# A fused LoRA and routed-adapter layer: A0's transposes, Bx's steps and a weight load change places in the prologue

## The chip, the cores and the metric

One core of a Trainium2 chip runs the kernel as one program. The metric is device time in microseconds (us). The profiled execution is a separate one, taken by the hardware profiler; its times are from the start of its span.

## The reference

x is 8 batches of 512 tokens by 2048, in float32. Two residual layers follow each other:

```
Bx  = x @ B0[adapter[b]].T                    # rank 16
x   = x + Bx @ A0[adapter[b]].T               # layer 0, a LoRA adapter chosen per batch
base   = x @ W.T                              # layer 1, W is 2048 x 2048
logits = x @ Wr.T + 5 * one_hot(language[b])  # 8 experts
gates  = softmax over the top 2 logits
h      = x @ A.T                              # 8 experts x rank 16 = 128 columns
x   = x + base + 2 * (h * gates) @ B.T
```

## The kernel before, in words

**How products are made.** Every float32 operand of a product is split into a high part (ScalarE casts it to fp32r) and a low part (VectorE subtracts), and TensorE sums three products of the parts (high by high, low by high, high by low; L820 to L822). TensorE's work for one batch is a list of slots, one for each pair of W's blocks. Batch 0 has 36 slots and works straight from W; batches 1 to 7 use sums of blocks that the slots of batch 0 prepare and store.

**The order is written by hand.** Each engine executes its own list of steps: `pe_start`, `act_start`, `dve_start`, `pool_start` and `sp_start` are the prologue, and `pe_main` and its fellows the slots. Engines meet only at semaphores, and an instruction that waits holds back all that stands behind it on its engine. SyncE (`sp_start`, `sp_main`) issues nearly all loads.

**The prologue.** It transposes x of batch 0 on TensorE in sixteen units (`x_transpose`, L319), ScalarE and VectorE take turns in copying a unit out of PSUM (`x_keep_act` L325, `x_keep_dve` L330), then `x_hi` (L350) and `x_lo` (L355) split it, and `aux_products` (L378, L380) multiplies it by the 152 columns of A, Wr and B0. The loop variable s in the lists is the step: at step s TensorE transposes unit 4 + s and multiplies unit s, while ScalarE and VectorE split unit 3 + s. After the last unit the sum of its second half is read (`aux_low` L390, `aux_sum` L395), and the sixteen columns of Bx go through `bx_hi` (L400, L401), `bx_lo` (L405), `bx_transpose` (L417) and `bx_keep` (L426), which leaves Bx in `bxt`.

**A0's part.** GpSimd orders A0 into `a0p`. `a0_transpose` 0 to 3 turns it (L1121), `a0_copy` (L1126, ScalarE) leaves it in `a0t`. `a0_rows_hi` (L1142, ScalarE) and `a0_rows_lo` (L1147, VectorE) split these rows in two halves; SyncE then sends the rows of batch 0 to `a0g` with three DMAs (L1407) and all rows to `a_scr` in memory with two (L1409). `a0_transpose` 4 to 7, `a0_hi` (L1131) and `a0_lo` (L1135) give the operand of `g_products` (L1157), sixteen tiles that multiply A0 by the same 152 columns.

**The first update of x.** `delta` (L533) is the product of `bxt` and `a0g` for one unit; it waits for `bxt` and for the rows in `a0g`. `adapt` (L540, VectorE) adds it to x, `first_hi` (L553) and `first_lo` (L558, called xl in the rows) split the new x. In slots 0 to 6 VectorE makes units 4 to 15 in this way, one or two in a slot. In the slots of batch 0 VectorE also turns a pair of W (`w_turn` L684, and L691 for blocks on the diagonal), forms two block sums (`w_sums`), and makes the low part of a pair (`pair_lo` L816) after ScalarE's high part (`pair_hi` L812). `first_products` of slot i waits for `pair_lo` of pair i, and at even i for units of `first_lo`. A pair of W is loaded by `first_load` (L669). GpSimd stores turned pairs and sums (`w_store`, `w_sums_store`), copies the second adapter's B into `bnj` (L1348), and makes two more block sums of each pair.

Of the kernel before, what the change touches and what calls it, by code (L numbers as in the profile page):

```python
# [5 lines left out]
def adapted_moe_lora_kernel(nc, x, adapter_ids, language_ids, A0, B0, W, Wr, A, Bm, out):  # L6
# [82 lines left out]
    with ctx:  # L89
# [1049 lines left out]
        def a0_rows_hi(e, half):  # L1139
            cols = slice(half * HO, (half + 1) * HO)  # L1140
            e.wait_ge(c_ac, 4)
            e.copy(arh[:, cols].bitcast(f32r), a0t[:, cols]).then_inc(c_arh, 1)  # L1142
# [79 lines left out]
        def pe_start(e):  # L1222
            warm(e, 18)
            for u in range(2):
                x_transpose(e, u)
            warm(e, 4)
            for m in range(2):
                a_transpose(e, m)
            small_transpose(e)
            for u in range(2, 4):  # L1230
                x_transpose(e, u)
            for s in range(16):
                if s < 12:
                    x_transpose(e, 4 + s)
                aux_products(e, 0, s)
                if 1 <= s < 3:
                    a_transpose(e, 1 + s)
                if 8 <= s < 16:
                    a0_transpose(e, s - 8)
            g_products(e, range(7))  # L1240
            bx_transpose(e, 0)
            g_products(e, range(7, 11))
            for u in range(2):
                delta(e, 0, u)
            g_products(e, range(11, 16))
            for u in range(2, 4):
                delta(e, 0, u)

        def act_start(e):
            x_load(e, 0, 0)  # L1250
            x_keep_act(e, 0)
            for u in range(2):
                x_hi(e, 0, u)
            for m in range(2):
                a_hi(e, m)
            small_hi(e)
            x_keep_act(e, 2)
            x_hi(e, 0, 2)
            for s in range(15):
                if s < 12 and s % 2 == 0:  # L1260
                    x_keep_act(e, 4 + s)
                if s == 8:
                    aux_low(e, 0, 0)
                if s < 13:
                    x_hi(e, 0, 3 + s)
                if 1 <= s < 3:
                    a_hi(e, 1 + s)
                if 8 <= s < 12:
                    a0_copy(e, s - 8)
                if s in (12, 13):  # L1270
                    a0_rows_hi(e, s - 12)
                if 12 <= s < 15:
                    a0_hi(e, s - 12)
                if s == 13:
                    pair_hi(e, 0)
            aux_low(e, 0, 1)
            a0_hi(e, 3)
            bx_hi(e, 0)
            pair_hi(e, 1)
            bx_keep(e, 0)  # L1280
            for u in range(2):
                first_hi(e, u)
            g_low(e)
            for u in range(2, 4):
                first_hi(e, u)
            g_hi(e)

        def dve_start(e):
            x_keep_dve(e, 1)
            for u in range(2):  # L1290
                x_lo(e, 0, u)
            for m in range(2):
                a_lo(e, m)
            small_lo(e)
            x_keep_dve(e, 3)
            x_lo(e, 0, 2)
            for s in range(15):
                if s < 12 and s % 2:
                    x_keep_dve(e, 4 + s)
                if s == 8:  # L1300
                    aux_sum(e, 0, 0)
                if s < 13:
                    x_lo(e, 0, 3 + s)
                if 1 <= s < 3:
                    a_lo(e, 1 + s)
                if s == 9:
                    bias_columns(e)
                if s in (12, 13):
                    a0_rows_lo(e, s - 12)
                if 12 <= s < 15:  # L1310
                    a0_lo(e, s - 12)
                if s in (9, 11):
                    w_turn(e, (s - 9) // 2)
            pair_lo(e, 0)
            aux_sum(e, 0, 1)
            a0_lo(e, 3)
            bx_lo(e, 0)
            w_sums(e, 0)
            pair_lo(e, 1)
            for u in range(2):  # L1320
                adapt(e, 0, u)
            for u in range(2):
                first_lo(e, u)
            for u in range(2, 4):
                adapt(e, 0, u)
            for u in range(2, 4):
                first_lo(e, u)
            g_sum(e)
            g_lo(e)
            w_turn(e, 2)  # L1330
            w_sums(e, 1)
# [43 lines left out]
        def sp_start(e):  # L1375
# [24 lines left out]
                first_load(e, g)  # L1400
            e.wait_ge(c_tr, 8)
            e.dma_start(bn, Bm.rearrange("e (p j) r -> p e j r", p=P)).then_inc(d_bn, 16)
            first_load(e, 3)
            e.wait_ge(c_ar, 2)
            e.wait_ge(c_pool, 5)
            for row, part in G_ROWS:
                e.dma_start(a0g[row:row + R, 0:D].bitcast(f32), (arh, arl)[part][0:R, :]).then_inc(d_ar, 16)  # L1407
            for s, t in enumerate((arh, arl)):
                e.dma_start(a_scr[s, :, 0:D], t).then_inc(d_as, 16)  # L1409
            first_load(e, 4)  # L1410
# [326 lines left out]
```

## Time and profile before

| | |
|---|---|
| median of 3 runs | 1571.99 us (1569.66 to 1574.66) |
| the profiled execution, its time | 1573.06 us |
| its span | 1571.3 us |
| TensorE busy | 1546.0 us (98%) |
| VectorE busy | 1225.4 us (78%) |
| ScalarE busy | 713.4 us (45%) |
| GpSimd busy | 138.9 us (9%) |
| granted TensorE clock, mean | 0.996 |
| bytes moved | 347.05 MB, 221 GB/s |

Busy time is the time in which an engine has an instruction under way; matmuls are pipelined, so a busy TensorE is not one at its peak. In a row of a timeline a square bracket gives the idle time of the engine ahead of the instruction and who ended it. The start of one instruction may lie up to 0.1 us ahead of the end of the one before it.

### The profile page before, as it was taken

Reading aid. Unit: us, or ns where it says so; the run is one execution under the profiler, and the core shown is the slowest. Engines: PE = TensorE matmul, PEld = TensorE weight load, DVE = VectorE, ACT = ScalarE, POOL = GpSimd, SP = SyncE. Lnnn points to the kernel's source line nnn. Section 1 sums busy time; section 2 is a strip of 40 time slices with the busy share of each in tenths; the row PEclk is TensorE's granted clock in tenths of the full one; section 3 lists DMA queues with packets and bytes.
Section 4 is the critical chain, followed back from the end, with each engine's and each line's share of the span. In section 5 each row is a group of like instructions: output and inputs, shape, how many; then the busy total and the mean of one; then the engine's idle time right before and its main releaser. Section 6 shows DMA issues by size and latency. Waiting matters only on the chain.

```text
span 1571.3 us, 20339 instructions
## 1 busy us (share of the span) xinstructions
PE 1546.0 (98%) x7430; PEld 1298.4 (83%) x7430; DVE 1225.4 (78%) x1630; ACT 713.4 (45%) x911; POOL 138.9 (9%) x181
## 2 busy tenths in 40 slices
PE   9989999999999999999999999999999999999998
PEld 9768877888888888888888888888888888888887
DVE  6987768877699777997688876987769976787665
ACT  6422222445445444454444544454444554445443
POOL 2565545000000000000000000000000000000000
PEclk9999999999999999999999999999999999999999
DMA  9799999687767777777776886668776786666664
GB/s 258 201 245 292 261 230 249 211 251 202 224 218 205 227 200 232 228 218 206 213 228 206 239 219 208 220 202 240 208 221 215 211 234 196 204 225 212 202 216 160
DMA packets 303110, 347.05 MB, mean 221 GB/s; under 512 B 204890, under 2 KB 236682, under 8 KB 302346
## 3 DMA queue, kind: packets, MB, share of 16 engines
q1 hardware_dynamic: 293602, 314.28, 69.1%
q0 software_dynamic: 9136, 30.94, 6.2%
q8 instruction: 59, 0.97, 0.3%
q10 hardware_dynamic: 272, 0.52, 0.1%
q14 instruction: 41, 0.34, 0.1%
HBM read 278.52 MB, written 66.72 MB: 220 GB/s over the span
## 4 chain that ended last, share of the span: by engine, by line
PE 90%; DVE 5%; DMA 2%; ACT 1%; issue 1%; SPq 1%; POOL 0%; DVEq 0%; ACTq 0%; POOLq 0%
PE pb L820 27%; PE pb L821 27%; PE pb L822 26%; PE pb L378 4%; PE pb L380 4%; PE pb L533 2%; DVE raw L684 1%; DVE xl L558 1%; DVE wl L816 1%; ACT wh L812 1%; DVE pool_a L540 1%; DMA t_scr<-ost 0%; DMA an<-in_L_cond_A_dram 0%; DMA raw<-in_L_cond_W_dram 0%; PE pb L319 0%
## 5 line engine op out<-in xcount | busy, mean ns | idle before, releaser
L812 ACT CAST wh<-raw 128x1024 fp32r<-128x1024 f32 (+1 forms) x453 | 475.1, 1049 | 716.9 <-PE pb L822 689.1
L816 DVE TENSOR_TENSOR wl<-raw,wh 128x1024 fp32r<-128x1024 f32 (+1 forms) x453 | 558.2, 1232 | 275.4 <-ACT wh L812 274.4
L820 PE MATMUL pb<-wh,sh 128*128 128x512 f32 x1568 | 612.9, 391 | 0.5 <-DVE ost L870 0.5
L821 PE MATMUL pb<-wl,sh 128*128 128x512 f32 x1568 | 611.7, 390 | 0.0
L822 PE MATMUL pb<-wh,sl 128*128 128x512 f32 x1568 | 611.1, 390 | 0.0
L822 PEld LDWEIGHTS pb<-wh,sl 128*128 128x128 f32 x1568 | 294.3, 188 | 62.9
L820 PEld LDWEIGHTS pb<-wh,sh 128*128 128x128 f32 x1568 | 294.5, 188 | 56.4 <-DVE wl L816 0.9
L821 PEld LDWEIGHTS pb<-wl,sh 128*128 128x128 f32 x1568 | 294.6, 188 | 55.0
L378 PE MATMUL pb<-awb,xah 128*128 128x304 f32 x512 | 139.3, 305 | 0.9 <-DVE xal L355 0.9
L380 PE MATMUL pb<-awb,xal 128*128 128x256 f32 x512 | 134.9, 280 | 0.0
L820 PE MATMUL pb<-wh,xh 128*128 128x512 f32 x256 | 102.2, 399 | 7.4 <-DVE xl L558 5.6
L378 PEld LDWEIGHTS pb<-awb,xah 128*128 128x128 f32 x512 | 96.9, 189 | 5.7 <-issue 1.3
L821 PE MATMUL pb<-wl,xh 128*128 128x512 f32 x256 | 101.1, 395 | 0.0
L822 PE MATMUL pb<-wh,xl 128*128 128x512 f32 x256 | 101.1, 395 | 0.0
L380 PEld LDWEIGHTS pb<-awb,xal 128*128 128x128 f32 x512 | 96.9, 189 | 4.1
L610 DVE TENSOR_TENSOR sl<-pool_a,sh 128x512 fp32r<-128x512 f32 x120 | 83.1, 693 | 0.3
L605 ACT CAST sh<-pool_a 128x512 fp32r<-128x512 f32 x120 | 73.5, 613 | 0.0
L350 ACT CAST xah<-pool_a 128x512 fp32r<-128x512 f32 x88 | 54.6, 621 | 28.8 <-DVE pool_a L277 27.9
L355 DVE TENSOR_TENSOR xal<-pool_a,xah 128x512 fp32r<-128x512 f32 x88 | 61.5, 699 | 3.5 <-ACT xah L350 3.3
L820 PEld LDWEIGHTS pb<-wh,xh 128*128 128x128 f32 x256 | 48.9, 191 | 18.1 <-DVE xl L558 4.0
L540 DVE TENSOR_TENSOR pool_a<-pool_a,pb 128x512 f32<-128x512 f32 x88 | 58.3, 677 | 1.0 <-PE pb L533 1.0
L533 PEld LDWEIGHTS pb<-bxt,a0g 128*128 128x128 f32 x256 | 45.1, 188 | 16.9 <-DVE pool_a L540 5.1
(155 smaller groups left out, 1298.0 us busy)
## 6 DMA issues: line engine op xcount, KB each, us to landing
raw<-t_scr SPq DMA_DIRECT2D x392, 512.0 KB, 3.9
xst<-in_x_dram SPq DMA_DIRECT2D x448, 64.0 KB, 3.9
out_dram<-ost SPq DMA_DIRECT2D x72, 256.0 KB, 3.6
raw<-in_L_cond_W_dram SPq DMA_DIRECT2D x124, 128.0 KB, 5.0
raw<-bt_scr SPq DMA_DIRECT2D x28, 512.0 KB, 3.6
out_dram<-u SPq DMA_DIRECT2D x56, 256.0 KB, 2.8
t_scr<-raw POOLq DMA_DIRECT2D x32, 256.0 KB, 4.6
t_scr<-tst POOLq DMA_DIRECT2D x16, 512.0 KB, 6.2
```

The source lines that it names most:

```text
L355: e.tensor_tensor(out=x_low(n, u).rearrange("p k t -> p (k t)"), in0=two(n, q, kp), in1=x_high(n, u).rearrange("p k t -> p (k t)").bitcast ...
L378: e.matmul(pb[:, aux_bank(n, u // 8) + t, 0:2 * AW], x_high(n, u)[:, k, toks], cols[:, 0:2 * AW], start=u % 8 == 0 and k == 0, stop=False)
L380: last = e.matmul(pb[:, aux_bank(n, u // 8) + t, 0:LOW], x_low(n, u)[:, k, toks], cols[:, 0:LOW], start=False, stop=u % 8 == 7 and k == 1)
L533: last = e.matmul(pb[:, delta_bank(n, u), k * HT:(k + 1) * HT], a0g[:, at:at + P], bxt[:, q // 2 * HT:(q // 2 + 1) * HT], start=True, stop ...
L540: e.tensor_tensor(out=two(n, q, kp), in0=two(n, q, kp), in1=pb[:, delta_bank(n, u), :], op=ALU.add)\
L605: e.copy(sh[:, h % SR, :, :].rearrange("p k t -> p (k t)"), two(b, SUM_QUARTER[product], kp)).then_inc(c_sph, 1)
L610: e.tensor_tensor(out=sl[:, h % SR, :, :].rearrange("p k t -> p (k t)"), in0=two(b, SUM_QUARTER[product], kp), in1=sh[:, h % SR, :, :].rea ...
L812: e.copy(pair_split(wh, g), pair_source(g)).then_inc(c_wh, 1)
L816: e.tensor_tensor(out=pair_split(wl, g), in0=pair_source(g), in1=pair_split(wh, g).bitcast(f32), op=ALU.subtract).then_inc(c_wl, 1)
L820: e.matmul(o, h, wh[:, g % RING, k, :], start=start, stop=False)
L821: e.matmul(o, h, wl[:, g % RING, k, :], start=False, stop=False)
L822: return e.matmul(o, l, wh[:, g % RING, k, :], start=False, stop=stop)
```

## The change

No instruction is added or taken away; instructions change places in four lists.

- TensorE: the eight groups of A0's transposes come at steps 5 to 8 and 10 to 13 instead of 8 to 15. `bx_transpose` comes after four tiles of `g_products` instead of seven, and the first two `delta` after eight instead of eleven.
- ScalarE: A0's copies and the splits of its rows move three steps ahead, `a0_hi` two or more. `pair_hi(0)` moves from step 13 to after the last step, still ahead of `aux_low(0, 1)`; `bx_keep` comes ahead of `pair_hi(1)`.
- VectorE: the splits of A0's rows move three steps ahead, `a0_lo` two or more. `w_turn` of pairs 0 and 1 moves from steps 9 and 11 to 12 and 14, `bias_columns` from step 9 to after the first `pair_lo`, `pair_lo(0)` to behind `bx_lo`, `pair_lo(1)` to behind the second two `adapt`, `w_sums(0)` to behind the fourth `first_lo`.
- SyncE: the load of pair 3 of W goes behind the rows of A0 and stands ahead of that of pair 4.

```diff
--- before.py
+++ after.py
@@ -1235,14 +1235,16 @@
                 aux_products(e, 0, s)
                 if 1 <= s < 3:
                     a_transpose(e, 1 + s)
-                if 8 <= s < 16:
-                    a0_transpose(e, s - 8)
-            g_products(e, range(7))
+                if 5 <= s < 9:
+                    a0_transpose(e, s - 5)
+                if 10 <= s < 14:
+                    a0_transpose(e, s - 6)
+            g_products(e, range(4))
             bx_transpose(e, 0)
-            g_products(e, range(7, 11))
+            g_products(e, range(4, 8))
             for u in range(2):
                 delta(e, 0, u)
-            g_products(e, range(11, 16))
+            g_products(e, range(8, 16))
             for u in range(2, 4):
                 delta(e, 0, u)
 
@@ -1265,19 +1267,17 @@
                     x_hi(e, 0, 3 + s)
                 if 1 <= s < 3:
                     a_hi(e, 1 + s)
-                if 8 <= s < 12:
-                    a0_copy(e, s - 8)
-                if s in (12, 13):
-                    a0_rows_hi(e, s - 12)
-                if 12 <= s < 15:
-                    a0_hi(e, s - 12)
-                if s == 13:
-                    pair_hi(e, 0)
+                if 5 <= s < 9:
+                    a0_copy(e, s - 5)
+                if s in (9, 10):
+                    a0_rows_hi(e, s - 9)
+                if 10 <= s < 14:
+                    a0_hi(e, s - 10)
+            pair_hi(e, 0)
             aux_low(e, 0, 1)
-            a0_hi(e, 3)
             bx_hi(e, 0)
+            bx_keep(e, 0)
             pair_hi(e, 1)
-            bx_keep(e, 0)
             for u in range(2):
                 first_hi(e, u)
             g_low(e)
@@ -1303,28 +1303,26 @@
                     x_lo(e, 0, 3 + s)
                 if 1 <= s < 3:
                     a_lo(e, 1 + s)
-                if s == 9:
-                    bias_columns(e)
-                if s in (12, 13):
-                    a0_rows_lo(e, s - 12)
-                if 12 <= s < 15:
-                    a0_lo(e, s - 12)
-                if s in (9, 11):
-                    w_turn(e, (s - 9) // 2)
+                if s in (9, 10):
+                    a0_rows_lo(e, s - 9)
+                if 10 <= s < 14:
+                    a0_lo(e, s - 10)
+                if s in (12, 14):
+                    w_turn(e, (s - 12) // 2)
+            aux_sum(e, 0, 1)
+            bx_lo(e, 0)
             pair_lo(e, 0)
-            aux_sum(e, 0, 1)
-            a0_lo(e, 3)
-            bx_lo(e, 0)
-            w_sums(e, 0)
-            pair_lo(e, 1)
+            bias_columns(e)
             for u in range(2):
                 adapt(e, 0, u)
             for u in range(2):
                 first_lo(e, u)
             for u in range(2, 4):
                 adapt(e, 0, u)
+            pair_lo(e, 1)
             for u in range(2, 4):
                 first_lo(e, u)
+            w_sums(e, 0)
             g_sum(e)
             g_lo(e)
             w_turn(e, 2)
@@ -1400,11 +1398,11 @@
                 first_load(e, g)
             e.wait_ge(c_tr, 8)
             e.dma_start(bn, Bm.rearrange("e (p j) r -> p e j r", p=P)).then_inc(d_bn, 16)
-            first_load(e, 3)
             e.wait_ge(c_ar, 2)
             e.wait_ge(c_pool, 5)
             for row, part in G_ROWS:
                 e.dma_start(a0g[row:row + R, 0:D].bitcast(f32), (arh, arl)[part][0:R, :]).then_inc(d_ar, 16)
+            first_load(e, 3)
             for s, t in enumerate((arh, arl)):
                 e.dma_start(a_scr[s, :, 0:D], t).then_inc(d_as, 16)
             first_load(e, 4)
```

## Rows read from the trace of the kernel before

**Rows 1.** The chain that ended last, piece from 42 us

```profile
42.02 5.08 DMA a0g<-a0p
```

**Rows 2.** Timeline of TensorE, 0 to 106 us: start, us, engine, line, operation [idle before]

```profile
22.69 0.63 PE L319 MATMUL pb<-ident,xst 128*128 128x128 f32 x4
...
24.18 0.63 PE L319 MATMUL pb<-ident,xst 128*128 128x128 f32 x4
...
28.68 0.60 PE L1121 MATMUL pb<-ident,a0p 128*128 128x128 f32 x4
...
30.62 0.60 PE L1121 MATMUL pb<-ident,a0p 128*128 128x128 f32 x4
...
41.75 0.39 PE L1157 MATMUL pb<-awb,a0h 128*128 128x304 f32 x1
...
44.23 0.66 PE L417 MATMUL pb<-ident,st 128*128 128x128 f32 x4 [0.28 <-DVE st L405]
...
47.24 0.71 PE L533 MATMUL pb<-bxt,a0g 128*128 128x256 f32 x4 [1.24 <-DMA a0g<-a0p]
...
50.56 0.47 PE L820 MATMUL pb<-wh,xh 128*128 128x512 f32 x1 [0.76 <-DVE xl L558]
...
84.14 0.52 PE L820 MATMUL pb<-wh,xh 128*128 128x512 f32 x1 [2.54 <-DVE xl L558]
...
103.78 0.50 PE L820 MATMUL pb<-wh,xh 128*128 128x512 f32 x1 [0.85 <-DVE xl L558]
```

**Rows 3.** Timeline of VectorE, 19 to 57 us

```profile
19.52 1.18 DVE L355 TENSOR_TENSOR xal<-pool_a,xah 128x512 fp32r<-128x512 f32 x1 [0.32 <-ACT xah L350]
...
25.99 0.69 DVE L355 TENSOR_TENSOR xal<-pool_a,xah 128x512 fp32r<-128x512 f32 x1 [1.11 <-ACT xah L350]
...
28.78 0.47 DVE L395 TENSOR_TENSOR aux<-pb,auxl 128x304 f32<-128x304 f32 x1 [0.90 <-ACT auxl L390]
...
30.97 0.69 DVE L355 TENSOR_TENSOR xal<-pool_a,xah 128x512 fp32r<-128x512 f32 x1 [0.38 <-ACT xah L350]
31.58 0.17 DVE L1215 CAST lidf<-lid 128x8 f32<-128x8 int32 x1
...
32.15 1.30 DVE L684 STREAM_TRANSPOSE raw<-raw 128x512 f32<-128x512 f32 x2
33.37 0.45 DVE L691 TENSOR_TENSOR raw<-raw,ident 128x128 f32<-128x128 f32 x2
...
37.74 1.22 DVE L1147 TENSOR_TENSOR a0p<-a0t,a0n 128x1024 fp32r<-128x1024 f32 x1
...
42.98 0.46 DVE L395 TENSOR_TENSOR aux<-pb,auxl 128x304 f32<-128x304 f32 x1
...
47.75 1.28 DVE L540 TENSOR_TENSOR pool_a<-pool_a,pb 128x512 f32<-128x512 f32 x2 [0.98 <-PE pb L533]
...
56.21 1.55 DVE L816 TENSOR_TENSOR wl<-raw,wh 128x1024 fp32r<-128x1024 f32 x1 [0.35 <-ACT wh L812]
```

**Rows 4.** Timeline of ScalarE, 29 to 46 us

```profile
29.32 1.20 ACT L1126 COPY a0t<-pb 128x512 f32<-128x512 f32 x1
30.25 0.69 ACT L350 CAST xah<-pool_a 128x512 fp32r<-128x512 f32 x1
...
36.62 1.05 ACT L1142 CAST a0n<-a0t 128x1024 fp32r<-128x1024 f32 x1
...
44.92 0.59 ACT L426 CAST bxt<-pb 128x512 fp32r<-128x512 f32 x1
```

**Rows 5.** SyncE's queue, 40 to 42 us

```profile
40.71 1.26 SPq L1407 DMA_DIRECT2D a0g<-a0n  x2
```

**Rows 6.** Timeline of GpSimd, 38 to 44 us

```profile
38.78 4.88 POOL L1348 COPY xst<-ost 128x256 f32<-128x256 f32 x8
```

**Rows 7.** Windows of TensorE in slots 3 and 4: busy us, granted clock, DMA share, GB/s

```profile
83.00:86.00 3.00, 1.86 (x5) 0.75 1.07 252
86.00:89.00 3.00, 3.00 (x11) 0.69 0.75 186
```

## The prediction

> **What bounds the kernel now.** I read the page first, then the chain that ended last, then the timelines of the five engines up to 106 us, and last the windows. The page says that TensorE is busy 98% of the span, so a change in the first 50 us can only shift the point from which it is always busy. The chain shows what sets that point. Up to 42 us it runs through the splits of A0's rows on VectorE and SyncE's queue, then through the landing of these rows [rows 1], and TensorE stands 1.24 us before the first delta [rows 2]. From there on it is VectorE's list, with short pieces of ScalarE: adapt, first_lo, w_turn, pair_lo, slot after slot. VectorE has no long idle time between 56 and 104 us; the typical one is the 0.35 us before a pair_lo [rows 3]. TensorE, which starts its slots at 50.56, is made to wait for xl 2.54 us at 84.14 and 0.85 us at 103.78 [rows 2]. After that last wait TensorE sets the pace. So what matters is not when the first delta starts but how late VectorE is when it leaves the prologue, which I read at its pair_lo of slot 0, 56.21 us [rows 3]. TensorE may be early or late by up to about 2.5 us in between; 84.14 takes it out.
>
> The same instructions run before and after on VectorE. So the result is a ledger of VectorE's idle time: whatever idle the new order adds ahead of that pair_lo is added to the end, whatever it removes is won. In before, from 24.8 us on, the idle times are 1.11, 0.90, 0.38 and 0.98 us [rows 3], 3.4 in all; the short ones after 50 us I take as common to both.
>
> **Prices.** A step of TensorE with transposes of x takes 1.49 us (22.69 to 24.18), one with A0's too 1.94 (28.68 to 30.62), so a group of A0's is 0.45 [rows 2]. VectorE: two instructions of 512 columns 1.30, so 0.61 apiece start to start; a w_turn with its two additions 1.6 (32.15 to 33.8); bias_columns 0.57 (31.58 to 32.15); 1024 columns 1.22, so about 1.13 start to start [rows 3]. ScalarE: a0_copy 0.93 (29.32 to 30.25), 512 columns about 0.5, 1024 columns about 0.95 [rows 4]. An engine sees another's result some 0.05 to 0.2 us after its end: a0_copy started at 29.32, the group of transposes having ended about 29.13.
>
> **Steps 5 to 8: A0's transposes and copies, three units sooner.** The first group starts at 24.18, where unit 10 was transposed [rows 2], and ends at 24.63. Four steps of 1.94 follow instead of 1.49; step 9 starts at 30.45. ScalarE takes the first copy at 24.8 and holds it to 25.75, the copy of unit 10 to 26.25, and only then x_hi of unit 9, complete at 26.85. VectorE waits for it from 24.8 to 26.9: 2.0 us idle after taking off the usual gap, where before it had 1.11. The next x_lo comes at 28.4, 0.3 idle. ScalarE's third copy runs 28.7 to 29.63, so aux_low comes at 30.15 and aux_sum at 30.6: 1.55 idle where it was 0.90. At these steps VectorE has 0.9 us of work in 1.94 and nothing to fill the rest. In before the longer steps were 8 to 11, and there w_turn and bias_columns filled them. This is the cost of the change.
>
> **Steps 9 to 14.** Steps 9 to 11 of TensorE end at 31.95, 33.9 and 35.8. ScalarE's a0_rows_hi run at 32.4 and 34.4, each behind an x_hi. VectorE's a0_rows_lo follow at 33.5 and 35.5 and end at 36.65; it waits 0.25 us each for x_lo of unit 12 and the two row halves, 0.7 together where it had 0.38. Then it has work without a break: a0_lo 0 to 37.3, the copy of unit 15 to 37.9, x_lo 14, a0_lo 1 to 39.1, x_lo 15 to 39.65, a0_lo 2 to 40.25, w_turn 0 to 41.85, a0_lo 3 to 42.45, w_turn 1 to 44.05. TensorE waits for a0_lo twice, about 0.55 and 0.25 us, and ends the sixteenth unit near 41.75, where the g_products started in before [rows 2]; the earlier A0 gives it nothing there.
>
> **The steps of Bx.** ScalarE has pair_hi(0) ahead of aux_low, and pair_hi(0) waits for w_turn 0 until 41.9: aux_low is complete at 43.35. VectorE is free of w_turn 1 only at 44.05, so aux_sum starts at 44.05 instead of 42.98. What follows is shorter, as a0_lo 3 no longer stands in it: bx_hi 44.55, bx_lo 45.0 (VectorE idle 0.5), bx_transpose 45.27 against 44.23, bx_keep 45.97 against 44.92, bxt complete at 46.6 against 45.51 [rows 2 to 4]. Behind bx_transpose stand four tiles of g_products, 1.1 us, to 46.8. The first delta is then at 46.8 instead of 47.24, 0.45 sooner.
>
> **The rows of A0 and pair 3.** SyncE gets both row halves at 36.7 instead of 40.71 [rows 5], 4 us sooner. The third DMA, 1.3 us on, would land at about 43.1 by the 5.08 us of before [rows 1]; even two more would do, as bxt comes at 46.6. So the wait of 1.24 us is gone, but bxt's lateness takes most of it. Pair 3 of W is loaded after the two stores to a_scr, and when w_turn 0 is done: about 41.9 to 44.6. It is wanted in slot 0 at some 63 us, so I cost this move at nothing; the bound above is small too, as 10 us of landing would still be in time. Pair 4 starts about 44.6, where it started 45.3. The sums of pair 0, a slot's worth later, are stored by GpSimd near 55 us; GpSimd then waits for w_turn 2 and the sums of pair 1 as before, and its last sum of pair 1 is ready near 60, ahead of w_turn 3. Nothing there is late.
>
> **VectorE up to slot 0.** From bx_lo: pair_lo(0) 45.15 to 46.3, bias_columns to 46.9, a wait of 0.35 for the delta, two adapt from 47.3 to 48.5, two first_lo to 49.9, a wait of 0.2 (TensorE has eight tiles of g_products, 2.25 us, ahead of the next two delta), two adapt to 51.35, pair_lo(1) to 52.5, two first_lo to 53.7, w_sums(0) to 55.15, the two steps of g to 56.0, w_turn 2 to 57.25, w_sums(1) to 58.05, and with the usual gap pair_lo at 58.45. It was 56.21. The ledger agrees: idle 2.0 + 0.3 + 1.55 + 0.7 + 0.5 + 0.35 + 0.2 = 5.6 us against 3.4, so VectorE is 2.2 us later. The 0.45 us gained at the delta is inside this: VectorE had idle time there, and now has work that it should have done earlier.
>
> **What covers it.** TensorE's first products need first_lo 0 and 1, at 49.9 against 50.3, and its second half first_lo 3, near 53.7 where it arrived at 53.9 before. So slot 0 starts as early as ever. But units 6 and 7 are 2.2 us late when TensorE wants them near 69 us, and the wait at 84.14 ends 2.2 us later. No slot from there to 103.78 has spare time on VectorE, so it all reaches the end: **+2.2 us**. On the profiled execution this is 1573.06 + 2.2 = 1575.3; on the median, 1.07 below that execution, 1571.99 + 2.2 = **1574.2 us**. A difference of 0.3%, 4.7 us, is about what a measurement of this kernel can tell from no change, so I forecast the same time, on the slow side of it.
>
> **The port of GpSimd, by row and rule.** The eight copies of B took GpSimd 38.78 to 43.66 [rows 6]. They wait behind the store of pair 1, which now follows w_turn 1, so they run 45.4 to 50.3, beside pair_lo(0) and two first_lo. An x_lo that ran beside a copy of GpSimd took 1.18 instead of 0.69 us [rows 3]. Three such meetings would cost 1.5 us; but the a0_rows_lo at 37.74 ran into the first of the eight and took 1.22, its ordinary length, so below the bound is 0. I take 0, since those are the same copies. The Trainium skill (GPSIMD Engine Reference, section Specifications) says that GpSimd shares its SBUF interfaces with VectorE and contends with VectorE instructions that have two SBUF inputs. By it the three would be slowed and the two adapt, with one input in PSUM, would not; the sum would be about 1575.7 on the median, and the row at 19.52 bears it out in part.
>
> **Rivals.** (1) *The gain reaches the end.* If ScalarE does not hold up x_hi in steps 5 to 8 (copies shorter, or VectorE's later waits for ScalarE short), the ledger ends level and the 0.98 us idle before the first adapt is what is removed: 1.0 to 1.2 us less, 1571.0. For it: the chain names the landing, 5.08 us of it [rows 1]. Against it: ScalarE's 0.93 us copy stands ahead of x_hi in its list, whatever else happens. (2) *The port*, as above: 0.5 to 1.5 us more, 1575. (3) *TensorE's clock falls, the case on the slow side.* TensorE now stands from 42.9 to 45.3 for bx_transpose, 2.4 us, since it has only four tiles to fill with. After the wait of 2.54 us the granted clock was 0.75 and 0.69 in two stretches of 3 us [rows 7]: it fell to half, 1.2 GHz, for 3.4 us of the six (0.25 and 0.31 lost, over 0.5), which costs 1.7 us of matmul work. Here the delta and g_products would carry it, VectorE waits for delta 2 until about 52, and is 1.8 us later again: +4.0, 1576.0. It passes 0.3% if the low stretch lasts longer than 4.8 us. For it: the similar wait. Against: 2.4 is shorter, and 1.24 us of waiting left the clock alone. (4) *The change does nothing*: the moved steps fall into idle time everywhere and the end stays, 1572.
>
> **How the numbers follow.** Forecast 0.5; (1) 0.18; (2) 0.12; (3) 0.12, half of whose weight is near or over the 0.3% line; (4) 0.08. The range reaches from (1) to beyond (3), widened by 1.5 us for the scatter of the median, which moved 5 us over three runs: 1569.6 to 1577.4. Slower by over 0.3% needs 1576.7: 0.09. Faster needs 1567.3, for which I find no mechanism, as all idle time that could go is 3.4 us: 0.03. The same: 0.88.
>
> **What the profile will show.** Right: VectorE's idle time before x_lo of unit 9 near 2 us and before aux_sum above 1.2; no wait of TensorE on the rows of A0; first delta near 46.8; pair_lo of slot 0 near 58.4; the wait of 2.5 us at 86.3. Wrong: that pair_lo at 56.2 or earlier means that the ledger was misread; a granted clock below 1 between 44 and 50 us means rival 3; first_lo above 1 us in the prologue, rival 2. If pair 3 arrived late there would be a VectorE wait on a load near 63 us.

## The result and the profile after

The changed kernel takes 1575.89 us, the median of 20 runs (1573.28 to 1580.73), against 1572.26 us for the kernel before (20 runs, 1569.13 to 1574.66). The ratio is 1.0026, with a 95% interval of 1.0020 to 1.0032: 3.6 us slower by the medians and 4.1 by the ratio, inside the 0.3% (4.7 us) that the prediction called no change, and on the side that it named. Its forecast was 2.2 us.

The profiled execution of the changed kernel has a span of 1573.8 us. TensorE's timeline, from the transposes of unit 9 and A0's first group, now behind them:

```profile
20.70 0.63 PE L319 MATMUL pb<-ident,xst 128*128 128x128 f32 x4
...
22.19 0.60 PE L1121 MATMUL pb<-ident,a0p 128*128 128x128 f32 x4
...
43.52 0.66 PE L417 MATMUL pb<-ident,st 128*128 128x128 f32 x4 [2.43 <-DVE st L405]
...
45.89 1.06 PE L533 MATMUL pb<-bxt,a0g 128*128 128x256 f32 x4
...
49.86 0.40 PE L820 MATMUL pb<-wh,xh 128*128 128x512 f32 x1
```

```profile
62.92 0.66 PE L1184 MATMUL pb<-ident,xst 128*128 128x128 f32 x4 [3.17 <-ACT bt L1189]
...
86.40 0.50 PE L820 MATMUL pb<-wh,xh 128*128 128x512 f32 x1 [2.53 <-DVE xl L558]
```

The wait for the rows of A0 is gone (45.89 has no bracket), and a wait of 2.43 us for bx_lo has come. The one in slot 4 has the length it had, 2.53 us, and ends 2.26 us later than in [rows 2] by the time of each trace. The wait of 3.17 us at 62.92 is new; ScalarE's copy of bt stands behind a first_hi that is late there. It is gone by 86.40, where TensorE waits for VectorE anyway.

VectorE's timeline, with lines that answer to [rows 3]:

```profile
24.96 0.69 DVE L355 TENSOR_TENSOR xal<-pool_a,xah 128x512 fp32r<-128x512 f32 x1 [1.42 <-ACT xah L350]
...
28.65 0.47 DVE L395 TENSOR_TENSOR aux<-pb,auxl 128x304 f32<-128x304 f32 x1 [1.48 <-ACT auxl L390]
...
30.69 0.69 DVE L355 TENSOR_TENSOR xal<-pool_a,xah 128x512 fp32r<-128x512 f32 x1 [0.24 <-ACT xah L350]
31.64 1.23 DVE L1147 TENSOR_TENSOR a0p<-a0t,a0n 128x1024 fp32r<-128x1024 f32 x1 [0.25 <-ACT a0n L1142]
...
38.32 1.30 DVE L684 STREAM_TRANSPOSE raw<-raw 128x512 f32<-128x512 f32 x2
...
40.51 1.30 DVE L684 STREAM_TRANSPOSE raw<-raw 128x512 f32<-128x512 f32 x2
...
42.10 0.47 DVE L395 TENSOR_TENSOR aux<-pb,auxl 128x304 f32<-128x304 f32 x1
43.03 0.44 DVE L405 TENSOR_TENSOR st<-aux,st 128x64 f32<-128x64 f32 x1 [0.46 <-ACT st L401]
43.39 1.42 DVE L816 TENSOR_TENSOR wl<-raw,wh 128x1024 fp32r<-128x1024 f32 x1
44.73 0.36 DVE L1215 CAST lidf<-lid 128x8 f32<-128x8 int32 x1
45.13 0.35 DVE L1217 TENSOR_TENSOR bias<-iota,lidf 128x64 f32<-128x64 f32 x1
45.52 0.28 DVE L1220 TENSOR_SCALAR bias<-bias 128x64 f32<-128x64 f32 x1
46.56 1.29 DVE L540 TENSOR_TENSOR pool_a<-pool_a,pb 128x512 f32<-128x512 f32 x2 [0.75 <-PE pb L533]
...
49.83 1.28 DVE L540 TENSOR_TENSOR pool_a<-pool_a,pb 128x512 f32<-128x512 f32 x2 [0.60 <-PE pb L533]
...
55.50 0.71 DVE L1176 TENSOR_TENSOR late<-late 128x136 fp32r<-128x136 f32 x1 [0.37 <-ACT late L1172]
...
58.54 1.55 DVE L816 TENSOR_TENSOR wl<-raw,wh 128x1024 fp32r<-128x1024 f32 x1 [0.35 <-ACT wh L812]
```

The idle times ahead of x_lo of unit 9 (24.96) and of aux_sum (28.65) have grown from 1.11 and 0.90 us to 1.42 and 1.48, the turns of pairs 0 and 1 run at 38.32 and 40.51 where they ran from 32.15, and the second aux_sum follows them at once. Behind it, bx_lo, pair_lo(0) and bias_columns (43.03 to 45.80) are all longer than the same instructions were, and each pair of adapt waits for its delta.

SyncE's queue and GpSimd's copies and next instruction, as in [rows 5, 6]:

```profile
34.84 1.26 SPq L1404 DMA_DIRECT2D a0g<-a0n  x2
...
40.03 1.91 SPq L669 DMA_DIRECT2D raw<-in_L_cond_W_dram  x4
41.98 0.60 SPq L1407 DMA_DIRECT2D a_scr<-a0n  x1
```

```profile
43.75 3.71 POOL L1346 COPY xst<-ost 128x256 f32<-128x256 f32 x8
...
55.98 0.82 POOL L738 TENSOR_TENSOR ost<-raw 128x256 f32<-128x256 f32 x1
```

The rows of A0 are sent 5.9 us sooner than in before (3.9 by the count from unit 9 that follows, where 4 was forecast), pair 3 goes out at 40.03 when w_turn 0 is done, and the copies of B start at 43.75 instead of 38.78, on top of bx_lo and pair_lo(0).

**One correction for how these two traces are compared.** Both kernels are the same up to the transposes of unit 9 in step 5, but the profiled execution of before had TensorE at half clock in step 0 and part of step 1 and that of the changed kernel had not. The windows of before and of after, from 13 to 16 us, with busy time of TensorE, granted clock, DMA share and GB/s:

```profile
13.00:16.00 3.00, 3.00 (x16) 0.50 1.08 360
```

```profile
13.00:16.00 3.00, 3.00 (x27) 1.00 1.08 362
...
44.00:46.00 2.00, 2.00 (x11) 0.55 1.09 381
46.00:48.00 2.00, 2.00 (x12) 0.60 0.99 408
```

So unit 9 is transposed at 22.69 in before and at 20.70 in after, 1.99 us apart with nothing changed ahead of it; 0.44 us of that are there at unit 4 already (12.62 and 12.18), ahead of the half clock, and the other 1.5 come in steps 0 and 1. From here on I count VectorE's lateness from these transposes: the pair_lo of slot 0 comes 56.21 - 22.69 = 33.52 us after them in before and 58.54 - 20.70 = 37.84 us in after, **4.3 us later**. That pair_lo came at 58.54 where 58.45 was forecast is chance, and so is the end of TensorE's wait at 86.40 where 86.3 was forecast: counted from unit 9 it is 4.25 us later than in before and not 2.2. At slot 8, where VectorE hands over, the low part of bt comes 80.95 and 85.18 us after unit 9, 4.2 us apart: all of it arrives. From there to the end of the span are 1467.7 and 1467.9 us; over the experiments this last part varies from 1466 to 1471 us with nothing changed in it, so a single execution can't decide about 2 us, and the lateness can.

### The profile page after: what moved, and what is told of

Its sections match the earlier page's. It is cut to its first block, busy times and chain, and to the rows that moved or that the text cites. A ratio compares the mean times of both kernels' runs of the same rounds, so it can differ in the third digit from the quotient of the medians.

```text
span 1573.8 us, 20339 instructions
## 1 busy us (share of the span) xinstructions
PE 1546.8 (98%) x7430; PEld 1300.1 (83%) x7430; DVE 1227.3 (78%) x1630; ACT 713.1 (45%) x911; POOL 138.2 (9%) x181
## 4 chain that ended last, share of the span: by engine, by line
PE 87%; SPq 4%; DVE 4%; DMA 1%; ACT 1%; issue 1%; DVEq 0%; POOL 0%; POOLq 0%; ACTq 0%
PE pb L821 25%; PE pb L820 25%; PE pb L822 25%; PE pb L378 4%; PE pb L380 3%; SPq L669 2%; PE pb L533 2%; SPq L292 2%; DVE raw L684 1%; DMA raw<-in_L_cond_W_dram 1%; DVE wl L816 1%; DVE xl L558 1%; ACT wh L812 1%; PE pb L319 0%; DMA xst<-in_x_dram 0%
## 5 line engine op out<-in xcount | busy, mean ns | idle before, releaser
L533 PEld LDWEIGHTS pb<-bxt,a0g 128*128 128x128 f32 x256 | 45.8, 192 | 15.0 <-DVE pool_a L540 5.6
```

The source lines that it names most:

```text
L533: last = e.matmul(pb[:, delta_bank(n, u), k * HT:(k + 1) * HT], a0g[:, at:at + P], bxt[:, q // 2 * HT:(q // 2 + 1) * HT], start=True, stop ...
```

## The experiments

The table has, for each kernel, the time from the transposes of unit 9 to VectorE's pair_lo of slot 0 in its profile ("late"), that difference to before, the median, and the ratio to the kernel before with its interval. The medians of before beside them were 1572.18 us (e1 to e4), 1571.57 (e5 to e8) and 1572.84 (e9 to e12).

| kernel | late, us | to before | median, us | ratio |
|---|---|---|---|---|
| before | 33.52 | | | |
| changed | 37.84 | +4.3 | 1575.89 | 1.0026 (1.0020 to 1.0032) |
| e1: A0's steps alone | 36.49 | +3.0 | 1574.62 | 1.0019 (1.0010 to 1.0028) |
| e2: seven tiles ahead of bx_transpose | 37.56 | +4.0 | 1575.06 | 1.0018 (1.0005 to 1.0030) |
| e3: the wait filled | 36.55 | +3.0 | 1575.82 | 1.0021 (1.0012 to 1.0030) |
| e4: turns back | 37.33 | +3.8 | 1575.48 | 1.0024 (1.0015 to 1.0033) |
| e5: first turn at step 8 | 35.39 | +1.9 | 1573.42 | 1.0010 (1.0001 to 1.0019) |
| e6: pair 3's load back | 43.69 | +10.2 | 1581.62 | 1.0058 (1.0044 to 1.0072) |
| e7: GpSimd's copies first | 37.77 | +4.3 | 1575.95 | 1.0029 (1.0019 to 1.0039) |
| e8: A0 one step sooner, turns at 8, 9 | 33.05 | -0.5 | 1571.44 | 1.0000 (0.9991 to 1.0009) |
| e9: e3 and e7 together | 36.21 | +2.7 | 1574.72 | 1.0011 (1.0001 to 1.0021) |
| e10: e5 and e7 together | 34.91 | +1.4 | 1572.70 | 0.9998 (0.9988 to 1.0008) |
| e11: e8 with another tail | 32.73 | -0.8 | 1572.56 | 0.9993 (0.9984 to 1.0003) |
| e12: pair 3 behind the rows, alone | 33.38 | -0.1 | 1572.30 | 0.9999 (0.9990 to 1.0007) |

Lateness and ratio mostly go together: kernels that are 3 us or more late take 3 us or more longer by their ratio (e2's is 2.8), those within 1 us of before can't be told from it. The intervals are some 1.5 us to either side, so the finer statements below rest on the profiles.

**e1, A0's steps alone.** The kernel before with only these moved (ScalarE's and VectorE's lists likewise):

```diff
-                if 8 <= s < 16:
-                    a0_transpose(e, s - 8)
+                if 5 <= s < 9:
+                    a0_transpose(e, s - 5)
+                if 10 <= s < 14:
+                    a0_transpose(e, s - 6)
```

> The kernel before, with A0's steps alone moved (transposes, copies, splits) and every other step where it was: w_turn at steps 9 and 11, bias_columns at 9, pair_hi(0) at 13, pair 3 of W ahead of the rows. Ledger theory: VectorE's idle time ahead of x_lo of unit 9 and of aux_sum grows from 1.1 and 0.9 us to about 1.4 and 1.5 as in the changed kernel, but the turns stand early again; VectorE's pair_lo of slot 0 then comes 1.0 to 1.5 us later than in the kernel before by the prologue's own clock, and the time is 1 to 1.5 us above before. Rival, that moving A0 is free and the moved turns alone cost: within 0.5 us of before. Rival, that the copies of ScalarE cost most: 2 us or more above before.

VectorE's idle time was as expected; its pair_lo was 3.0 us late, not 1 to 1.5. The idle times ahead of x_lo of unit 9 and of aux_sum, and a row that nobody had expected:

```profile
24.69 0.69 DVE L355 TENSOR_TENSOR xal<-pool_a,xah 128x512 fp32r<-128x512 f32 x1 [1.43 <-ACT xah L350]
...
28.37 0.47 DVE L395 TENSOR_TENSOR aux<-pb,auxl 128x304 f32<-128x304 f32 x1 [1.48 <-ACT auxl L390]
```

```profile
41.91 2.96 DVE L816 TENSOR_TENSOR wl<-raw,wh 128x1024 fp32r<-128x1024 f32 x1
```

```profile
41.70 3.77 POOL L1348 COPY xst<-ost 128x256 f32<-128x256 f32 x8
```

This pair_lo took 2.96 us beside GpSimd's eight copies; in before it took 1.25. So 1.7 of the 3.0 us are a meeting of VectorE and GpSimd, and about 1.1 are idle time. That moving A0 is free is refuted. The turn at step 9 also holds up a0_lo here, so that TensorE waits 2.05 us ahead of a group of A0's transposes and its granted clock is 0.50 from 38 to 40 us; behind the long pair_lo this cost nothing, as aux_sum had no wait.

**e4, the turns back in the changed kernel.**

```diff
-                if s in (12, 14):
-                    w_turn(e, (s - 12) // 2)
+                if s in (9, 11):
+                    w_turn(e, (s - 9) // 2)
```

(and bias_columns at step 9.)

> The changed kernel with w_turn of pairs 0 and 1 back at steps 9 and 11 and bias_columns at 9. Ledger theory: VectorE's idle time of steps 5 to 8 is ahead of step 9 and is not filled by this, so that the total of its idle time hardly falls (0 to 0.5 us gained); the turns then hold up the splits of A0's rows and x_lo 14, 15 instead. Rival, that the late turns themselves are the cost, through the steps of Bx: aux_sum comes about 2 us sooner and the time falls by 2 us or more from the changed kernel's 1575.9, to that of before.

0.5 us less late, the time the same within the interval: the rival, 2 us or more, didn't come. But the run is no clean test of the turns' place, since the turn at step 9 brings a cost of its own, as in e1. TensorE waits for a0_lo, which now stands behind that turn, its granted clock is 0.50 from 38 to 40 us and 0.71 to 42, and here the second aux_sum waits for its products:

```profile
37.07 0.66 PE L1121 MATMUL pb<-ident,a0t 128*128 128x128 f32 x4 [2.05 <-DVE a0l L1135]
```

```profile
43.29 0.47 DVE L395 TENSOR_TENSOR aux<-pb,auxl 128x304 f32<-128x304 f32 x1 [1.10 <-ACT auxl L390]
```

Without these 1.10 us the kernel would be some 2.7 us late (an estimate, all else as it is) and not 3.8, so how much the place of the turns at steps 12 and 14 costs, between 0.5 and 1.6 us, isn't settled. What is shown is that turns at 9 and 11 don't undo the change; the idle time of steps 5 to 8 is ahead of them.

**e5, the first turn where VectorE stood idle.**

```diff
                 if s == 8:
+                    w_turn(e, 0)
                     aux_sum(e, 0, 0)
```

(and its place at step 12 is empty.)

> The changed kernel with w_turn of pair 0 at step 8, ahead of aux_sum, where VectorE stood idle for 1.48 us, and w_turn of pair 1 where the change has it. Ledger theory: the idle time is filled, aux_sum of the second half comes 1.3 to 1.6 us sooner, and VectorE's pair_lo of slot 0 is 1.2 to 1.6 us sooner against the transposes of unit 9; the time falls by as much, to about 1574.4. Rival, that pair 0 has not landed by then: VectorE waits for a load at step 8 and nothing is won. Rival, that idle time on VectorE at these steps is not what counts: no change of the time.

```profile
28.82 1.30 DVE L684 STREAM_TRANSPOSE raw<-raw 128x512 f32<-128x512 f32 x2
...
30.46 0.47 DVE L395 TENSOR_TENSOR aux<-pb,auxl 128x304 f32<-128x304 f32 x1
...
42.59 0.47 DVE L395 TENSOR_TENSOR aux<-pb,auxl 128x304 f32<-128x304 f32 x1
```

The turn runs where the 1.48 us were, and aux_sum of unit 7's half has no wait left. The kernel is 2.45 us less late, more than the turn's 1.6, since the steps of Bx come sooner and TensorE's wait ahead of bx_transpose shrinks to 1.11 us, after which its clock stayed at full. The ledger is borne out, and pair 0 had landed. The time bears it out too: this ratio's interval ends at 1.0019, just below where that of the changed kernel begins (1.0020).

**e3, TensorE's wait filled.**

```diff
             g_products(e, range(4))
+            for m in range(20):
+                e.transpose(pb[:, 5, m % 4 * P:(m % 4 + 1) * P], ident[:, :], ident[:, :])
             bx_transpose(e, 0)
```

> The changed kernel with twenty transposes of the identity into a free bank ahead of bx_transpose, in TensorE's wait of 2.43 us; their result is not used. Clock theory: the granted clock stays at full from 44 to 47.5 us, where it was half, the second two delta come about 1.2 us sooner, VectorE's idle time of 0.60 us ahead of the second pair of adapt is gone with part of the 0.75 ahead of the first, and the time falls 0.8 to 1.3 us below the changed kernel's, to about 1574.9. Rival, that the low clock is hidden behind VectorE: the clock stays full and the time stays at 1575.9 within 0.4.

The granted clock stayed at 1.00 where the changed kernel had 0.55 and 0.60 (with the same wait of 2.43 us in e6 it was 0.52 from 46 to 48 us; filled once more, in e9, it stayed at 1.00), and VectorE had no bracket ahead of either pair of adapt:

```profile
47.48 1.27 DVE L540 TENSOR_TENSOR pool_a<-pool_a,pb 128x512 f32<-128x512 f32 x2
...
50.30 1.27 DVE L540 TENSOR_TENSOR pool_a<-pool_a,pb 128x512 f32<-128x512 f32 x2
```

1.3 us less late, the upper end of what was expected. The median of the times did not follow (1575.82; the interval of its ratio reaches from 1.9 to 4.7 us above before): one profile shows the cost, the timing doesn't confirm it.

**e2, seven tiles instead of four.**

```diff
-            g_products(e, range(4))
+            g_products(e, range(7))
             bx_transpose(e, 0)
-            g_products(e, range(4, 8))
+            g_products(e, range(7, 8))
```

> The changed kernel with seven tiles of g_products ahead of bx_transpose instead of four (0.84 us more work in the wait), as it was before. Clock theory: the wait falls from 2.43 to 1.6 us, the clock stays full, and three tiles less stand ahead of the first delta: both pairs of adapt come 0.5 to 1.2 us sooner and the time is 0.8 to 1.3 us below the changed kernel's. Rival, that a low clock after the wait is hidden: no difference within 0.4 us.

A miss: the wait was 1.59 us as expected, but the clock still fell, 0.53 and 0.62 from 46 to 50 us, behind a further wait of 0.40 us for bxt, and the kernel is as late as the changed one within 0.3 us. The first delta was in time, the second pair of adapt waited 0.93 us instead. The low stretch had only moved.

**e7, GpSimd's copies first.**

```diff
-            w_store(e, 0)
-            w_store(e, 1)
             e.wait_ge(d_bn, 16)
             for m in range(E):
                 e.tensor_copy(bnj[:, :, m * R:(m + 1) * R], bn[:, m, :, :]).then_inc(c_bnj, 1)
+            w_store(e, 0)
+            w_store(e, 1)
```

> The changed kernel with GpSimd's eight copies of B ahead of its stores of pairs 0 and 1 of W instead of behind them. Port theory: the copies run from about 36 to 40 us, away from bx_lo, pair_lo(0) and bias_columns, whose lengths fall back from 0.44, 1.42 and 0.36, 0.35, 0.28 us to 0.21, 1.22 and 0.17, 0.23, 0.20; the first delta is 0.3 us sooner and pair_lo of slot 0 0.5 to 0.9 us sooner, unless the copies now lengthen x_lo or a0_rows_lo by as much. Rival, that these lengths come from the loads in flight and not from GpSimd: they stay.

```profile
44.04 0.23 DVE L405 TENSOR_TENSOR st<-aux,st 128x64 f32<-128x64 f32 x1 [0.46 <-ACT st L401]
44.18 1.22 DVE L816 TENSOR_TENSOR wl<-raw,wh 128x1024 fp32r<-128x1024 f32 x1
45.32 0.17 DVE L1215 CAST lidf<-lid 128x8 f32<-128x8 int32 x1
45.52 0.22 DVE L1217 TENSOR_TENSOR bias<-iota,lidf 128x64 f32<-128x64 f32 x1
45.77 0.19 DVE L1220 TENSOR_SCALAR bias<-bias 128x64 f32<-128x64 f32 x1
47.85 1.28 DVE L540 TENSOR_TENSOR pool_a<-pool_a,pb 128x512 f32<-128x512 f32 x2 [1.88 <-PE pb L533]
```

The lengths are the ordinary ones again (0.23, 1.22, 0.17, 0.22, 0.19), so the longer ones were GpSimd's doing and not that of loads in flight. One x_lo beside the moved copies took 0.82 for 0.69; in all VectorE is busy 0.7 us less than in the changed kernel. But VectorE, sooner ready, now stands 1.88 us for a delta that TensorE makes at half clock (0.61 and 0.53 from 44 to 48 us), and the kernel is as late as before this edit. One cost had hidden the other. In part it is also a worse case of the same cost: the clock had fallen before bx_transpose here, which took 1.04 us for 0.66.

**e9, both taken away.** The edits of e3 and e7 together, in part:

```diff
+            for m in range(20):
+                e.transpose(pb[:, 5, m % 4 * P:(m % 4 + 1) * P], ident[:, :], ident[:, :])
             bx_transpose(e, 0)
...
-            w_store(e, 0)
-            w_store(e, 1)
             e.wait_ge(d_bn, 16)
```

> The changed kernel with both the twenty transposes of the identity ahead of bx_transpose and GpSimd's copies ahead of its stores. With the copies alone VectorE's instructions had their ordinary lengths again, but it then stood 1.88 us for a delta that TensorE made at half clock, and nothing was won. Theory that the two costs hide each other: with both taken away the first delta follows bxt at once, and pair_lo of slot 0 is 0.5 to 1.0 us sooner, against the transposes of unit 9, than with the transposes alone (36.55), and 1.8 to 2.3 us sooner than in the changed kernel (37.84). Rival, that a third thing holds the first delta (the landing of A0's rows): at 36.5 as with the transposes alone.

1.6 us less late than the changed kernel, and 0.3 less than with the transposes alone; 1.8 to 2.3 and 0.5 to 1.0 were expected. The direction holds, the size was too large: 0.40 us of waiting for the first delta is left, because four tiles still stand ahead of it. What remains of the 4.3 us, 2.7, is 1.0 by which x_lo of unit 9 starts later, 0.9 of further idle time (the wait for aux_sum above all) and 0.8 of busy time, of which the second step of g is 0.4.

**e10, the turn at step 8 and the copies first.** The edits of e5 and e7 together, in part:

```diff
                 if s == 8:
+                    w_turn(e, 0)
...
-            w_store(e, 0)
-            w_store(e, 1)
             e.wait_ge(d_bn, 16)
```

> The changed kernel with w_turn of pair 0 at step 8 and GpSimd's copies ahead of its stores. The turn alone gave pair_lo of slot 0 at 35.39 us after the transposes of unit 9, against 37.84 changed and 33.52 before. Port theory: 0.5 to 1.0 us less, 34.4 to 34.9, and a time 1 to 1.5 us above before. Rival, as with the copies alone: the lengths fall back, but the first delta does not come sooner, and pair_lo stays at 35.4.

34.91, the upper end of what the port theory gave, and a time that can't be told from before (0.9998) and is clear of the changed kernel's. With the idle time filled and the copies elsewhere, what the change cost is gone within the noise.

**e6, the load of pair 3 ahead of the rows again.**

```diff
+            first_load(e, 3)
             e.wait_ge(c_ar, 2)
             e.wait_ge(c_pool, 5)
             for row, part in G_ROWS:
                 e.dma_start(a0g[row:row + R, 0:D].bitcast(f32), (arh, arl)[part][0:R, :]).then_inc(d_ar, 16)
-            first_load(e, 3)
```

> The changed kernel with the load of pair 3 of W ahead of the rows of A0 again. It waits for w_turn 0, at 40 us, so the rows are sent at about 42 instead of 34.8 and land near 47. Theory that this order is needed once the turns are late: TensorE waits some 1 us for the rows, the first adapt comes 1 us later and the time is 0.5 to 1 us above the changed kernel's. Rival, that the order of these loads costs or gives nothing: within 0.4 us.

The largest miss, 5.9 us above the changed kernel by the lateness. The chain that ended last:

```profile
41.50 0.31 SPq L669
...
43.52 0.65 SPq L1405
...
44.83 7.01 DMA a0g<-a0p
...
51.97 1.20 PE pb L533 x4
```

SyncE waits for w_turn 0, issues pair 3, and sends the rows at 43.5 to 45.8. The third of the three DMAs took 7.0 us to land, beside pair 3 and GpSimd's stores of pairs 0 and 1, and not the 5.08 of [rows 1] that I had used. TensorE stands 4.75 us, works at half clock until 56, and VectorE waits 5.49 us for the first delta. Once the turns are late this move is needed.

**e12, the move of the change alone, in the kernel before.**

```diff
-            first_load(e, 3)
             e.wait_ge(c_ar, 2)
...
+            first_load(e, 3)
             for s, t in enumerate((arh, arl)):
```

> The kernel before with the load of pair 3 of W behind the rows of A0, as the change has it, and nothing else. The rows cannot be sent sooner than 40.7 us, as VectorE has them then; pair 3 is loaded at about 42.6 instead of 33.9 and is wanted at 61. Theory that the order matters only where the turns are late: the time stays within 0.4 us of before, with the rows at most 1 us sooner for having the rings to themselves, which would take some of the 1.24 us before the first delta. Rival: pair 3 or pair 4 comes late and VectorE waits for a load in slots 0 or 1: 1 us or more above before.

As expected: no difference. TensorE waits 1.10 us for the rows where it waited 1.24.

**e8 and e11, less idle time from the kernel before.** A0 one step sooner instead of three (ScalarE's and VectorE's lists likewise), and both turns where VectorE waits:

```diff
-                if 8 <= s < 16:
-                    a0_transpose(e, s - 8)
+                if 7 <= s < 15:
+                    a0_transpose(e, s - 7)
...
                 if s == 8:
+                    w_turn(e, 0)
                     aux_sum(e, 0, 0)
...
-                if s in (9, 11):
-                    w_turn(e, (s - 9) // 2)
+                if s == 9:
+                    w_turn(e, 1)
```

> The kernel before with A0's steps one step sooner (transposes at 7 to 14) and w_turn of pair 0 at step 8 ahead of aux_sum, of pair 1 at 9; nothing else moved. Ledger theory: the turn fills VectorE's idle time ahead of aux_sum, the rows of A0 land sooner so that the idle time of 0.98 us ahead of the first adapt shrinks, and pair_lo of slot 0 comes 1 to 2 us sooner than in the kernel before: 1570.2 to 1571.2, faster than both. Rival, that ScalarE's a0_copy ahead of x_hi costs as much as it wins: within 0.5 us of before. Rival, the port: GpSimd's copies meet pair_lo(0), which then takes up to 3 us, and the time is 1 us or more above before.

Late by 0.5 us less than before and not by 1 to 2: VectorE waited 0.65 us for pair 0 to land, and 0.77 for a0_hi 3. The time is that of before. e11 moves a0_lo(3) into the wait for bx_lo:

```diff
             aux_sum(e, 0, 1)
+            a0_lo(e, 3)
```

> The kernel before with A0's steps one step sooner and w_turn at 8 and 9, and besides a0_lo(3) behind aux_sum of the second half, where VectorE stood 0.46 us idle for bx_lo, instead of ahead of pair_lo(0), where it stood 0.77. Ledger theory: 0.8 to 1.2 us less idle, pair_lo of slot 0 at 32.0 after the transposes of unit 9 (33.05 without it, 33.52 before), the time 1 to 1.5 us below before. Rival: the first delta then waits for A0's rows, which SyncE sends at 39.4, and VectorE's idle time only moves there: 33.0.

```profile
46.43 0.71 PE L533 MATMUL pb<-bxt,a0g 128*128 128x256 f32 x4 [0.65 <-DMA a0g<-a0p]
```

0.3 us less, not 1: the first delta waited for A0's rows again, 0.65 us, as the rival had it. At 0.9993 it has the lowest ratio of all, but its interval holds 1, so no version here is shown to beat the kernel before.

## Why the prediction was right, point by point

**The frame held.** The pace is VectorE's until slot 8, its lateness reaches the end undiminished (4.3 us at slot 0, 4.2 at slot 8, 3.6 in the median). TensorE's slots don't start "as early as ever": 49.86 is 29.16 us after unit 9, where it was 27.87, but 1.3 us is little enough for the wait at 86.40 to take it out. The ratio lies in the range, and the outcome was the one given 0.88; the forecast of 2.2 us was 1.4 short of the medians' 3.6, and the terms that were too small are below.

**Steps 5 to 8, right in their delay.** x_lo of unit 9 started 3.30 us after the transposes of unit 9 in before and 4.26 in after, 0.96 more where 0.9 was worked out; ahead of aux_sum 1.48 us of idle time for 1.55; the next three 0.22, 0.24 and 0.25. e5 shows that filling it gives it back. The idle time ahead of that x_lo was 1.42 us and not near 2, since VectorE was less far ahead: two x_lo beside GpSimd's ordering of A0 had taken 2.64 us (19.70). In e2, e3, e7 and e10 that meeting fell otherwise, and with the same start, 4.26, the idle time was 2.07 or 2.08. So the sum of the prediction's idle times, 5.4 us for 5.6, looks better than it was: 0.6 too much here hides 0.8 too little at the two pairs of adapt. That is luck.

**Two terms of the sum were mis-sized, both in one direction.** From x_lo of unit 9 to pair_lo of slot 0, busy time of VectorE in a window of that length, of before and of after:

```profile
25.98:56.21 30.23, 26.88 (x50) 1.00 1.01 232
```

```profile
24.95:58.54 33.59, 28.47 (x51) 0.95 0.85 207
```

Idle time is 3.35 and 5.12 us, so with the 0.96 it grew by 2.7 us, not 2.2. Busy time grew by 1.6 us, not 0. Together 4.3.

- *The first delta, "0.45 sooner".* It came 24.55 us after unit 9 in before and 25.19 in after, 0.64 later. TensorE made the eight matmuls of its four tiles after bx_transpose in 1.95 us (43.94 to 45.89) at a granted clock of 0.55, for which I had 1.1. The idle times ahead of the two pairs of adapt were 0.75 and 0.60, not 0.35 and 0.2. This is rival 3's mechanism; I had given it 0.12 and cost it at 1.8 us. e3's profile puts it at 1.3.
- *The port, "I take 0".* It cost up to 1.2 of the 1.6 us of busy time, inside the bound of 1.5, and on other instructions than the first_lo of rival 2: bx_lo 0.44 for 0.21, pair_lo(0) 1.42 for 1.25, the three instructions of bias_columns 0.99 together for 0.60, and the second step of g 0.71 for 0.30. e7 shows the cause, for the first three, by taking it away: 0.8 us. Beside the second step of g lie GpSimd's store at 55.21 and its block sum at 55.98; no run moved these, so that 0.4 isn't shown. The other 0.4 of the 1.6 can't be tied to GpSimd: it is spread over the rows in hundredths and in overlaps of one instruction's start with the end of the one before. My reason for 0, that the same copies had met the same kind of instruction before at no cost, rested on a row that overlapped them by 0.2 us only (37.74 to 38.96, the copies from 38.78 on). The next one in before lay in their midst and was of ordinary length too:

```profile
39.48 1.21 DVE L1147 TENSOR_TENSOR a0p<-a0t,a0n 128x1024 fp32r<-128x1024 f32 x1
```

The conclusion for the new places was wrong all the same. The Trainium skill (GPSIMD Engine Reference, section Specifications) names contention with VectorE instructions that have two SBUF inputs or run in a 2-port perf mode. pair_lo has two; lidf in bias_columns, a cast with one input, also doubled, from 0.17 to 0.36, and no view here shows the mode it ran in.
- *The two don't add.* e3 alone gives 1.3, e7 alone 0.1, both 1.6 us. With GpSimd's copies away TensorE, at half clock, still sets the first adapt; with the clock at full VectorE, slowed by GpSimd, sets it itself. That is why rivals priced one at a time were poor guides here.

**Pair 3, wrong as told, without effect on the sum.** I had it loaded behind the two stores to a_scr; it stands ahead of them, behind the rows, and was issued at 40.03, the stores at 41.98. And I cost the move at nothing by asking when pair 3 is wanted. The right question was what would happen without it: 5.9 us (e6).

**Rivals.** (1), a gain that reaches the end, is out: no run that has A0 three steps sooner is shown ahead of before (the best, e10, has 1 in its interval), and ScalarE's copy ahead of x_hi did what was said against it. (2) and (3) both happened in part. (4) is out.

**What stays open.** What of the half clock happens in each of the twenty timed executions isn't known, since only one of each kernel has a trace; and the length of a wait alone doesn't tell whether the clock falls (the last section has waits of 3.2 us of both kinds); the 4.3 us of that one and the 3.6 of the median differ by less than the scatter of the last part. Why pair_lo took 2.96 us beside the copies in e1, 1.42 in the changed kernel and 1.25 in before isn't settled: it began 0.2 us after the copies in e1, 0.4 us ahead of them in the changed kernel and in their midst in before.

## What to carry to other kernels

Where an engine other than the busiest sets the point from which the busiest is saturated, count that engine's idle time in both orders and not the one wait at the head of the chain: a step moved sooner leaves its cost where it went, here 2.7 us of idle time against 1.24 us of waiting removed. Work that fills an idle stretch must move with it (e5: 1.6 us of work moved back, 2.45 us won). And price what a new wait does to its neighbours, above all to TensorE's clock and to which instructions then run side by side with GpSimd's, together and not one at a time.

## What the runs showed of the hardware

- In the prologue TensorE's granted clock fell to half, 1.2 GHz, after waits of 2.43 us (changed, e6), 2.21 (e7), 2.05 (e1, e4) and 1.59 with 0.40 more soon after it (e2), and stayed at 2.4 GHz after waits of 1.48 (e1), 1.11 (e5) and 0.89 us (e10).
- In the slots the same length went both ways. After the wait of 3.17 us that ends at 62.92 the changed kernel had 1.00, and after 3.18 us e9 had 0.50 from 62 to 66; after 2.53 us at 86.40 the changed kernel had 1.00 again, and after 2.54 at 84.14 before had 0.57 from 84 to 88. The window of the changed kernel behind 62.92:

```profile
62.00:66.00 4.00, 3.08 (x18) 1.00 0.42 132
```

- In the same, unchanged steps 0 and 1 the clock was at half from 13 to 16 us in some executions (0.50 in before) and at full in others (1.00 in after), which shifts all that follows by some 1.5 us.
- A VectorE subtraction of 1024 columns, 1.22 us by itself, took 2.96 us beside eight GpSimd copies that together took 3.77 us (e1), and 1.25 in the midst of eight that took 4.88 (before).
- A copy of A0's rows of 128 KB landed 5.08 us after its issue in before and 7.0 us in e6, with other transfers issued just ahead of it.
